# Small unused writes between GpSimd's indirect transfers in a two-layer transformer kernel

## The chip, the cores and the metric

The kernel runs on one core of a Trainium2 chip. The metric is device time in microseconds (us). It is one program with one launch, and its engines are TensorE (PE), VectorE (DVE), ScalarE (ACT), GpSimd (POOL) and SyncE (SP), which work in parallel and wait for one another on semaphores.

## The reference

1024 tokens of width 256 pass through four stages. Each adds its result to its input and normalises the sum.

```
x = layernorm(x + attention(x))          # 16 heads, causal, latent keys of rank 64
x = layernorm(x + experts0(x))           # 64 experts, top 8, at most 128 tokens each
x = layernorm(x + recurrence(x))         # state = tanh(f) * state + g, along the sequence
x = layernorm(x + experts1(x) + shared(x))   # 8 experts, top 2, and one shared MLP

experts0: logits = x @ router.T; the 8 largest probabilities of a token, divided by their sum, weigh
          the outputs of its 8 experts; a token's place in its expert's queue is a running count;
          expert e: silu(xe @ gate) * (xe @ up) @ down      (256 -> 96 -> 256)
experts1: 2 largest of 8, softmax of the two; expert e: silu(x @ w1a) * (x @ w1b) @ w2   (256 -> 512 -> 256)
shared:   silu(x @ w_gate) * (x @ w_up) @ w_down          (256 -> 1024 -> 256)
```

Everything is in float32.

## The kernel before, in words

The tokens form 8 tiles of 128. Every engine runs its own hand-written program, and its order is the order of the code; no scheduler moves anything. GpSimd's program matters here. It does small arithmetic (splitting queries into a high and a low part at L696 and L698, the inverse roots of the layer norms at L703), and it issues all transfers whose addresses depend on the data. Such an indirect transfer takes an index for each of 128 rows out of a tile and moves 128 rows of 1 KB, between on-chip memory and a table in HBM. There are four kinds:

- **First sends** (`send`, L705 to L709). When a tile's attention output is normalised (`x1_rows`), its top 8 experts are known (`send_i`), and eight transfers write its rows into `xe_d`, the table from which experts0 reads. Tiles 0 to 5 issue one transfer in every second slot of the following tile's attention, between splits. The seventh tile (`t == TILES - 2`) issues one a slot, in a stretch where no splits are left, and the last tile issues its eight in one go once attention has ended. After the last tile's k-th send SP loads expert k's rows (the keys are sorted, so expert k's rows are complete by then), and PE starts on expert 0.
- **Home sends** (`send_home`, L733 to L739), one for each of 64 experts, write expert outputs to `ye_d`. The change leaves them alone.
- **Second sends** (L774 to L778): 16 transfers write the rows for experts1 into `xd_d`. SP waits for all of them, then loads the first block of rows. At that time PE computes the shared MLP for the first half of the tokens (`shared_in`, then `shared_out`, L1979); its fourth quarter is preceded by the transposition of the first block (`block_T`, L1988), for which those rows are needed.
- **Final gathers** (L781 to L784): 16 transfers read each token's two expert outputs back from `yd_d`. Meanwhile PE computes the shared MLP's second half (L1625 to L1627), ACT its silu (L957), DVE the product (L1424), and after the third, fourth and further products DVE adds a tile's gathered rows (`last_sum`, L1560 and L1562). Four variances follow and then the last norms.

The inverse root of the last tile (`rstd_of(TILES - 1)`, L703) stands in GpSimd's program behind the seventh tile's sends; behind it come that tile's norm, its routing and its sends.

Of the kernel before, what the change touches and what calls it, by code (L numbers as in the profile page):

```python
# [6 lines left out]
P = 128  # L7
T, HID = 1024, 256
TILES = T // P
# [7 lines left out]
E0, TOP0, CAP, I0 = 64, 8, 128, 96  # L17
# [19 lines left out]
def build(nc, x, xT, wq, wq_ropeT, wkv_aT, kv_ln, wkv_b, woT, router0T, gate_up0, down0, w_in, init_state,  # L37
# [5 lines left out]
    with ctx:  # L43
        def sb(name, shape, dt=f32):
            return ctx.enter_context(nc.sbuf_tensor(name, shape, dt))

        def sem(name):
            return ctx.enter_context(nc.semaphore(name))
# [60 lines left out]
        rsum = sb("rsum", [P, 3, QUAD])  # L109
        rinv = sb("rinv", [P, 3, QUAD])  # L110
        y = sb("y", [P, HID])
        sgd = sb("sgd", [P, 2, BANK])
        ctxT = sgd
        stats = sb("stats", [P, 6])
# [111 lines left out]
        def out_of(n):  # L226
# [28 lines left out]
            sem(n) for n in ("zeroed", "x1T_psd", "x1T_done", "logits_done", "logits_read", "chosen_done",  # L255
                             "place_done", "place_read", "send_done"))
        sent = [sem(f"sent0_{u}") for u in range(2)]
        last_sends = sem("last_sends")
        consts0, route_step, exp_ready, exp_done, winv_done = (
            sem(n) for n in ("consts0", "route_step", "exp_ready", "exp_done", "winv_done"))  # L260
# [118 lines left out]
        def tile_of(G):  # L379
            return G // SETS  # L380
# [269 lines left out]
        def _(pool):  # L650
# [39 lines left out]
            def split_q(m):  # L690

                qt, h = divmod(2 * m, HEADS)
                two = qT[:, h * T:(h + 2) * T].rearrange("p (h t) -> p h t", h=2)[:, :, qt * P:(qt + 1) * P]
                if m >= 3:
                    pool.wait_ge(scores_ready, 2 * (m - 3) + 2)
                pool.tensor_copy(q_his[m % 3], two).then_inc(q_half, 1)  # L696
                pool.wait_ge(q_half, m + 1)
                pool.tensor_tensor(q_los[m % 3], two, q_his[m % 3].bitcast(f32), ALU.subtract).then_inc(q_split, 1)  # L698

            def rstd_of(k, s=0):  # L700

                pool.wait_ge(var_done, k + 1)
                pool.tensor_tensor(rstd[:, s:s + 1], mv[:, s, 1:2], minus_half[:, 0:1], ALU.pow).then_inc(rstd_done, 1)  # L703

            def send(t, k):  # L705
                pool.wait_ge(send_done, t + 1)
                pool.wait_ge(exp_done, t + 1)
                pool.indirect_dma_start(xe_d, bass.IndirectOffsetOnAxis(send_i[:, t, k:k + 1], 0), x1_rows[:, t, :],  # L708
                                        None).then_inc(sent[k % 2] if t < TILES - 1 else sent_last[k], 16)  # L709
# [7 lines left out]
            def pool_slot(G, i, n):  # L717
                if n % 2 == 0 and n // 2 + 3 < TILES * PAIRS:
                    split_q(n // 2 + 3)
                t, at = divmod(n - 2 * HEADS, HEADS)  # L720
                if t == 0 and at == 0:
                    pool.wait_ge(homes_made, 2)
                    pool.wait_ge(rows_zeroed, 16 * ROWS_ZEROED)
                if 0 <= t < TILES - 1 and (t < TILES - 2 and at % 2 or t == TILES - 2 and at < TOP0):
                    send(t, at // 2 if t < TILES - 2 else at)
                if SETS + 2 <= G < GROUPS and (G % SETS, i) == (2, 0):
                    rstd_of(tile_of(G) - 1)
            head_slots(pool_slot)
            rstd_of(TILES - 1)
            for k in range(TOP0):  # L730
                send(TILES - 1, k)
                pool.sem_inc(last_sends, 1)

            def send_home(e, u):

                hold(pool, ye_done, e + 1)
                hold(pool, home_done, e + 2 - u % 2)
                pool.indirect_dma_start(ye_d, bass.IndirectOffsetOnAxis(home_i[:, u:u + 1], 0),  # L738
                                        ye[:, u, :], None).then_inc(moved[u], 16)  # L739
# [35 lines left out]
            for t in range(TILES):  # L775
                for k in range(TOP1):
                    pool.indirect_dma_start(xd_d, bass.IndirectOffsetOnAxis(slot1[:, t, k:k + 1], 0),
                                            x1[:, t, :], None).then_inc(sent1, 16)  # L778
            pool.wait_ge(st_yd[0], 16 * (BLOCKS - BLOCKS // 2))
            pool.wait_ge(st_yd[1], 16 * (BLOCKS // 2))  # L780
            for t in range(TILES):  # L781
                for k in range(TOP1):
                    pool.indirect_dma_start(last_rows[:, t, k, :], None, yd_d,  # L783
                                            bass.IndirectOffsetOnAxis(slot1[:, t, k:k + 1], 0)).then_inc(moved[t], 16)  # L784
            for t in range(TILES // 2):
                rstd_of(3 * TILES + t, t)

# [1321 lines left out]
```

## Time and profile before

| | us |
|---|---|
| median of 3 runs | 816.11 |
| lowest and highest run | 810.94 and 816.73 |
| profiled execution, first to last instruction | 851.6 |
| mean granted clock of PE in it | 0.982 |

The profiled execution's own span is 35.5 us longer than the median run. Only that execution has a trace, so every duration below is one of it.

### The profile page before, as it was taken

How to read it: one execution, taken by the hardware profiler on the slowest of the kernel's cores; microseconds unless marked ns; L12 is line 12 of the kernel's file. 1: busy time of each engine (PE TensorE's matmuls, PEld its weight loads, DVE VectorE, ACT ScalarE, POOL GpSimd, SP SyncE). 2: the span in 40 equal slices, each digit the busy share in tenths (PEclk: the TensorE clock that was granted, in tenths of full speed). 3: DMA queues.
4: the chain of work that ended last, by engine and by line, in shares of the span. 5: the costliest groups of instructions: out<-in, count | busy, mean ns of one | idle time of the engine just before them, and what ended most of it. 6: DMA issues, size and time to landing. Idle time of an engine off the chain costs nothing.

```text
span 851.6 us, 16159 instructions
## 1 busy us (share of the span) xinstructions
PE 786.6 (92%) x4635; PEld 660.7 (78%) x4635; DVE 556.9 (65%) x1423; ACT 394.8 (46%) x898; POOL 271.2 (32%) x357
## 2 busy tenths in 40 slices
PE   8998999999899999999879998899999799999957
PEld 7887877778787887777677877788897688888746
DVE  4324778877778787777345555468856387778536
ACT  1334656656565666655123343323333266666411
POOL 2004445534333232222345545524415100000241
PEclk9999999999999999999889999999999999999979
DMA  7449950000000000073176999687621335555321
GB/s 212 102 107 384 406 198 34 34 27 27 21 27 28 20 21 14 27 240 135 51 230 184 323 319 296 213 288 257 246 99 69 106 112 150 149 149 153 95 69 49
DMA packets 62881, 120.74 MB, mean 142 GB/s; under 512 B 18272, under 2 KB 32864, under 8 KB 62688
## 3 DMA queue, kind: packets, MB, share of 16 engines
q1 hardware_dynamic: 51824, 95.41, 35.2%
q0 software_dynamic: 7680, 21.51, 7.0%
q10 hardware_dynamic: 3312, 3.02, 1.0%
q8 instruction: 33, 0.54, 0.3%
q14 instruction: 32, 0.26, 0.1%
HBM read 76.13 MB, written 43.78 MB: 141 GB/s over the span
## 4 chain that ended last, share of the span: by engine, by line
PE 65%; DVE 11%; issue 11%; ACT 4%; POOL 3%; another core or an unknown queue 3%; DMA 2%; DVEq 0%; SPq 0%; ACTq 0%; POOLq 0%
PE scores L1627 9%; PE scores L1625 8%; PE scores L1626 8%; PE scores L1849 5%; PE acc_ps L2035 4%; PE misc_ps L1755 3%; PE probsT_ps L1762 3%; PE probsT_ps L1740 3%; PE misc_ps L1753 3%; DVE xT_lo L1096 3%; PE scores L1859 3%; PE acc_ps L1740 2%; PE probsT_ps L1979 2%; DVE neg_max L1090 2%
## 5 line engine op out<-in xcount | busy, mean ns | idle before, releaser
L826 ACT ACTIVATE area<-scores,neg_max 128x128 f32<-128x128 f32 (+7 forms) x128 | 94.9, 742 | 87.7 <-DVE neg_max L1090 85.5
L1090 DVE TENSOR_REDUCE neg_max<-scores 128x1 f32<-128x128 f32 (+7 forms) x128 | 95.8, 750 | 22.1 <-PE scores L1712 20.8
L708 POOL DMA_INDIRECT xe_d<-x_rows,send_i x64 | 64.1, 1001 | 55.5 <-ACT x_rows L850 38.5
L738 POOL DMA_INDIRECT ye_d<-area,home_i x64 | 61.4, 959 | 58.7 <-issue 28.6
L1849 PE MATMUL scores<-area 128*96 128x128 f32 x512 | 69.1, 279 | 2.1 <-issue 1.3
L1625 PE MATMUL scores<-kT_hi,weff_hi 128*128 128x512 f32 (+3 forms) x172 | 66.8, 388 | 0.9 <-ACT area L803 0.4
L1849 PEld LDWEIGHTS scores<-area 128*96 128x96 f32 x512 | 60.5, 166 | 5.2 <-issue 2.7
L1627 PE MATMUL scores<-kT_hi,weff_lo 128*128 128x512 f32 (+3 forms) x172 | 61.7, 359 | 0.0
L1626 PE MATMUL scores<-kT_lo,weff_hi 128*128 128x512 f32 (+3 forms) x172 | 61.5, 358 | 0.0
L696 POOL CAST weff_hi<-area 128x256 fp32r<-128x256 f32 x42 | 17.0, 406 | 136.5 <-PE scores L1712 88.8
L1755 PE MATMUL misc_ps<-xT_lo,xT_hi 128*128 128x512 f32 x144 | 58.4, 406 | 2.2 <-DVE xT_lo L1096 2.1
L783 POOL DMA_INDIRECT area<-yd_d,slot x16 | 15.3, 955 | 141.0 <-DMA yd_d<-area 136.4
L1740 PE MATMUL probsT_ps<-ident,area 128*128 128x128 f32 x320 | 48.6, 276 | 5.3 <-DVE xT_lo L1096 5.1
L1762 PE MATMUL probsT_ps<-area,sgd 128*128 128x256 f32 x162 | 50.5, 395 | 1.3 <-ACT sgd L839 0.9
L1859 PE MATMUL scores<-area 96*128 96x256 f32 x128 | 40.6, 399 | 11.0 <-DVE area L1268 9.6
L874 ACT ACTIVATE area<-scores 96x128 f32<-96x128 f32 x64 | 17.3, 271 | 67.7 <-PE scores L1849 40.3
L1096 DVE TENSOR_TENSOR xT_lo<-probsT_ps,xT_hi 128x512 fp32r<-128x512 f32 x53 | 36.1, 686 | 18.5 <-ACT xT_hi L833 17.5
L1753 PE MATMUL misc_ps<-xT_hi 128*128 128x512 f32 x96 | 47.4, 494 | 0.1
L1625 PE MATMUL scores<-xT_hi,weff_hi 128*128 128x512 f32 x110 | 46.1, 419 | 0.0
L1268 DVE TENSOR_TENSOR area<-area,scores 96x128 f32<-96x128 f32 x64 | 18.0, 282 | 41.1 <-ACT area L874 26.1
L1740 PEld LDWEIGHTS probsT_ps<-ident,area 128*128 128x128 f32 x320 | 36.0, 143 | 11.1 <-issue 8.1
L2035 PE MATMUL acc_ps<-area 128*128 128x256 f32 x184 | 43.5, 379 | 0.8 <-DVE area L1511 0.8
(290 smaller groups left out, 2081.4 us busy)
## 6 DMA issues: line engine op xcount, KB each, us to landing
area<-w SPq DMA_DIRECT2D x23, 512.0 KB, 4.0
area<-gate_up SPq DMA_DIRECT2D x24, 384.0 KB
xe_d<-area SPq DMA_DIRECT2D x8, 1088.0 KB, 11.3
ye_d<-area SPq DMA_DIRECT2D x8, 1024.0 KB, 16.7
area<-w SPq DMA_DIRECT2D x8, 1024.0 KB, 7.2
area<-ye_d SPq DMA_DIRECT2D x15, 512.0 KB, 5.2
area<-xe_d SPq DMA_DIRECT2D x28, 272.0 KB
area<-down SPq DMA_DIRECT2D x24, 192.0 KB
```

What stands on the lines that cost most here:

```text
L826: act.activation(row_of(n)[:, 0:L], score_bank(n)[:, 0:L], ACT.Exp, bias=neg_max[:, n % 4:n % 4 + 1], accum_out=rsum[:, s, k:k + 1]).then_ ...
L1090: dve.tensor_reduce(neg_max[:, n % 4:n % 4 + 1], score_bank(n)[:, 0:(n // HEADS + 1) * P], AX.X, ALU.max, negate=True).then_inc(max_ready, 1)
L1625: pe.matmul(out_ap, lh, rh, start=start, stop=False)
L1626: pe.matmul(out_ap, lh, rl, start=False, stop=False)
L1627: return pe.matmul(out_ap, ll, rh, start=False, stop=stop)
L1740: last = pe.transpose(seat_of("block", b)[:, i * P:(i + 1) * P], row_of(QUAD * G + i)[:, k * P:(k + 1) * P], ident[:])
L1753: pe.matmul(ctx_ps[:], latent[:, k, :], pT_hi[b % 3], start=k == 0, stop=False)
L1755: pe.matmul(ctx_ps[:], latent[:, k, :], pT_lo[b % 3], start=False, stop=k == tile_of(G)).then_inc(ctx_step, 1)
L1762: pe.matmul(out_of(n), ctxT[:, G % 2, i * P:(i + 1) * P], wvo[:, h * HID:(h + 1) * HID], start=True, stop=True).then_inc(out_ready, 1)
L1849: last = pe.matmul(half[b][0:I0, part * P:(part + 1) * P], weights_of(e)[0][:, c, part * I0:(part + 1) * I0], xeT[:, b, c, :], start=c == ...
L1859: pe.matmul(half[2 + b][:, 0:HID], hT[:, b, :], weights_of(e)[1], start=True, stop=True).then_inc(ye_ps, 1)
L2035: last = pe.matmul(acc[:, 0:HID], hdT[:, u, c * P:(c + 1) * P], w2_b[:, u, c, :], start=c == 0, stop=c == I1 // P - 1)
```

## The change

A tile `breath` of 128 x 256 is added, and a helper that sets some of its columns to zero and then makes GpSimd wait for its own write. Nothing reads the tile. The helper is called after each of the seventh tile's eight sends (twice, 256 columns), after the last tile's sends except the eighth (128 columns), after each of the 16 second sends (128 columns) and after each of the 16 final gathers (256 columns). That is 16 + 7 + 16 + 16 = 55 writes. The instructions that were there keep their order on every engine.

```diff
+        breath = sb("breath", [P, HID])
...
+            def breathe(columns):
+
+                pool.memset(breath[:, 0:columns], 0.0).then_inc(breathed, 1)
+                breaths[0] += 1
+                pool.wait_ge(breathed, breaths[0])
...
                     send(t, at // 2 if t < TILES - 2 else at)
+                    if t == TILES - 2:
+                        breathe(HID)
+                        breathe(HID)
...
             for k in range(TOP0):
                 send(TILES - 1, k)
                 pool.sem_inc(last_sends, 1)
+                if k < TOP0 - 1:
+                    breathe(P)
...
                     pool.indirect_dma_start(xd_d, bass.IndirectOffsetOnAxis(slot1[:, t, k:k + 1], 0),
                                             x1[:, t, :], None).then_inc(sent1, 16)
+                    breathe(P)
...
                     pool.indirect_dma_start(last_rows[:, t, k, :], None, yd_d,
                                             bass.IndirectOffsetOnAxis(slot1[:, t, k:k + 1], 0)).then_inc(moved[t], 16)
+                    breathe(HID)
```

GpSimd's own program around the seventh and the last tile's sends, before. The names after the operation are the tile written and the tiles read, in brackets stand the semaphores waited for, and x12 is twelve alike in a row (the last four of the sixth tile and the eight of the seventh):

```order
L703 TENSOR_TENSOR rstd<-mv,minus_half 128x1 [waits var_done]
L708 DMA xe_d<-x_rows,send_i 65536x272 [waits exp_done,send_done] x12
L703 TENSOR_TENSOR rstd<-mv,minus_half 128x1 [waits var_done]
L708 DMA xe_d<-x_rows,send_i 65536x272 [waits exp_done,send_done] x8
L738 DMA ye_d<-area,home_i 16384x256 [waits zeroed,ye_done,home_done]
```

The same place in the changed kernel, from the seventh tile's last send on (L718 is the send, L705 the inverse root):

```order
L718 DMA xe_d<-x_rows,send_i 65536x272 [waits exp_done,send_done,breathed]
L711 MEMSET breath 128x256
L711 MEMSET breath 128x256 [waits breathed]
L705 TENSOR_TENSOR rstd<-mv,minus_half 128x1 [waits var_done,breathed]
L718 DMA xe_d<-x_rows,send_i 65536x272 [waits exp_done,send_done]
L711 MEMSET breath 128x128
L718 DMA xe_d<-x_rows,send_i 65536x272 [waits exp_done,send_done,breathed]
```

Two writes now stand between the seventh tile's sends and ahead of the last tile's inverse root, and one between the last tile's sends; each transfer behind a write waits for `breathed`.

GpSimd's program at the second sends and the final gathers, before:

```order
L703 TENSOR_TENSOR rstd<-mv,minus_half 128x1 [waits var_done]
L777 DMA xd_d<-x_rows,slot 2944x256 [waits slots1_ready]
L777 DMA xd_d<-x_rows,slot 2944x256 x15
L783 DMA area<-yd_d,slot 128x256 [waits st_yd1,st_yd0]
L783 DMA area<-yd_d,slot 128x256 x15
L703 TENSOR_TENSOR rstd<-mv,minus_half 128x1 [waits var_done] x4
```

In the changed kernel, from the last second send on (L792 is the second send, L799 the gather):

```order
L792 DMA xd_d<-x_rows,slot 2944x256 [waits breathed]
L711 MEMSET breath 128x128
L799 DMA area<-yd_d,slot 128x256 [waits st_yd1,st_yd0,breathed]
L711 MEMSET breath 128x256
L799 DMA area<-yd_d,slot 128x256 [waits breathed]
```

The two runs of 16 transfers are no longer unbroken: a write with its wait stands after every one.

## Rows read from the trace of the kernel before

**Rows 1.** The page: the span, and each engine's busy time, share and instructions.
```profile
span 851.6 us, 16159 instructions
PE 786.6 (92%) x4635; PEld 660.7 (78%) x4635; DVE 556.9 (65%) x1423; ACT 394.8 (46%) x898; POOL 271.2 (32%) x357
```

**Rows 2.** The chain that ended last: start, length (us) and what it is.
```profile
405.29 2.10 issue
...
421.62 11.12 another core or an unknown queue
...
460.83 2.31 another core or an unknown queue
...
659.91 7.21 another core or an unknown queue
...
813.86 8.99 issue
```

**Rows 3.** Timeline, last tile's sends: start, us, engine, what, [idle before <-releaser].
```profile
420.88 0.17 DVE L1189 TENSOR_SCALAR send_i<-keys_i 128x8 int32<-128x8 int32 x1
421.34 1.04 POOL L708 DMA_INDIRECT xe_d<-x_rows,send_i  x1 [5.08 <-DVE send_i L1189]
...
427.75 1.04 PE L1849 MATMUL scores<-area 128*96 128x128 f32 x8
...
430.26 0.96 POOL L708 DMA_INDIRECT xe_d<-x_rows,send_i  x1 [0.30 <-issue]
432.77 0.44 ACT L874 ACTIVATE area<-scores 96x128 f32<-96x128 f32 x2 [11.14 <-remote]
```

**Rows 4.** Timeline, second sends and the first block of experts1.
```profile
663.70 0.96 POOL L777 DMA_INDIRECT xd_d<-x_rows,slot  x1 [0.30 <-issue]
666.17 0.81 SPq L614 DMA_DIRECT2D area<-xd_d  x2
...
672.96 0.38 PE L1988 MATMUL misc_ps<-ident,area 128*128 128x128 f32 x2
```

**Rows 5.** Timeline, final gathers and the shared MLP's second half.
```profile
812.25 0.39 PE L1627 MATMUL scores<-xT_hi,kT_lo 128*128 128x512 f32 x1
...
819.99 0.95 POOL L783 DMA_INDIRECT area<-yd_d,slot  x1 [0.30 <-issue]
822.23 0.60 ACT L957 ACTIVATE sgd<-scores 128x512 f32<-128x512 f32 x1 [10.08 <-remote]
...
824.27 0.80 PE L1625 MATMUL scores<-xT_hi,kT_hi 128*128 128x512 f32 x1 [8.21 <-DVE kT_lo L1410]
...
835.27 0.48 DVE L1560 SCALAR_TENSOR_TENSOR area<-area,weight,x_rows 128x256 f32<-128x256 f32 x1
```

**Rows 6.** Windows: PE, PEld, DVE, ACT, POOL busy us (count); granted clock, DMA share, GB/s.
```profile
432.60:439.50 6.90, 6.09 (x24) 5.51 (x25) 2.71 (x12) 1.66 (x5) 1.43 (x2) 0.51 0.73 205
...
818.30:828.50 10.20, 4.23 (x10) 3.36 (x11) 4.39 (x10) 2.39 (x6) 2.02 (x3) 0.50 0.14 43
```

**Rows 7.** Groups and timeline: GpSimd's writes, a send among splits, a home send.
```profile
L662 POOL MEMSET area<- 128x1024 f32 x1 | 1.0, 952 | 0.0
...
L651 POOL MEMSET ident<- 128x128 f32 x1 | 0.2, 204 | 0.3 <-POOLq L2099 0.3
...
122.07 1.01 POOL L708 DMA_INDIRECT xe_d<-x_rows,send_i  x1 [0.15 <-issue]
123.08 0.41 POOL L696 CAST q_hi<-area 128x256 fp32r<-128x256 f32 x1
...
437.65 0.47 ACT L881 ACTIVATE area<-scores,hw 128x256 f32<-128x256 f32 x1 [0.58 <-PE scores L1859]
439.03 0.96 POOL L738 DMA_INDIRECT ye_d<-area,home_i  x1 [2.04 <-ACT area L881]
```

**Rows 8.** Timeline of GpSimd: the seventh tile's first send and the inverse root behind its sends.
```profile
398.22 0.96 POOL L708 DMA_INDIRECT xe_d<-x_rows,send_i  x1 [24.01 <-ACT x_rows L850]
...
415.69 0.57 POOL L703 TENSOR_TENSOR rstd<-mv,minus_half 128x1 f32<-128x1 f32 x1 [7.66 <-DVE mv L1122]
```

More of the change, by code:

```diff
@@ L257, in build @@
         sent = [sem(f"sent0_{u}") for u in range(2)]
+        breathed = sem("breathed")
         last_sends = sem("last_sends")
@@ L703, in rstd_of @@
                 pool.tensor_tensor(rstd[:, s:s + 1], mv[:, s, 1:2], minus_half[:, 0:1], ALU.pow).then_inc(rstd_done, 1)
+            breaths = [0]
+            def breathe(columns):
+                pool.memset(breath[:, 0:columns], 0.0).then_inc(breathed, 1)
+                breaths[0] += 1
+                pool.wait_ge(breathed, breaths[0])
             def send(t, k):
```

## The prediction

> **What bounds the kernel.** The page comes first: PE is busy in 92% of an 851.6 us span [rows 1], so time is lost where PE is made to stand, and GpSimd, busy in 32%, matters only where somebody waits for it. The chain of waits comes next. Most of it is work; I looked for long pieces that are none, and four of the longest lie beside the four runs of indirect transfers that the change touches: 2.10 us from 405.29, 11.12 from 421.62, 7.21 from 659.91 and 8.99 from 813.86 [rows 2]. The timeline of such a piece shows what it is. PE ends expert 0's gate and up products at 428.79 (427.75 + 1.04), and ACT, which has nothing else to do, starts on them at 432.77; the row calls the releaser "remote", which is to say that no record of the increment was found [rows 3]. GpSimd's eighth send ended at 431.22, 1.55 us ahead. It is the same with the gathers: PE's chunk ends at 812.65, ACT starts on it at 822.23, 1.29 us after GpSimd's last gather has ended at 820.94 [rows 5]. At the second sends the chain stands from 659.91 to 667.12, and GpSimd's last send ended at 664.66 [rows 2, 4]. So in the profiled execution PE's signals to ACT and DVE are held back while GpSimd issues indirect transfers one behind another, and come when the run is over. The hold isn't there from the start of a run: the piece at 659.91 begins some 15 us after the first of those sends (663.70 less 15 intervals of 1.26 is 644.8).
>
> **What the holds cost there.** At the last tile 432.77 - 428.79 = 4.0 us, and then PE works at a granted 0.51 (the 1.2 GHz level) from 432.6 to 439.5, 6.09 us busy [rows 6], of which half, 3.0, is lost: 7.0. At the seventh tile 2.1 [rows 2], and a stretch at the lower clock behind it, for which I take somewhat less than the last tile's 3.0, since part of it is idle filler: 4.5 in all. At the second sends the first block's rows can't be loaded before 666.17, when SP has seen all sends land, 2.47 us after the last one started at 663.70 [rows 4]; with 2.5 us for the load as well, PE could transpose at 668.7 instead of 672.96, and with a slower load at 670: 3 to 4, say 3.5. At the gathers PE stands 8.21 us before 824.27, and half of 4.23 us at clock 0.50 is 2.1 [rows 5, 6]: 10.3. Together 25.3 us. In experts0 the chain has four more such pieces, 2.31 us at 460.83 and three alike of 2.33 to 2.42 [rows 2], 9.4 us in all, and the change adds nothing there. All holds make 34.7 us.
>
> **Where I chose: are the holds in the timed runs?** The profiled execution took 851.6 us first to last instruction, the median of the timed runs is 816.11. That is 35.5 us less, though a time holds all that the span holds. The holds add up to 34.7, nearly the same. The simplest reading is that the timed runs hold back few of PE's signals or none: what is slow is the recorded execution. The missing records of the increments speak for that too: recording is what is overloaded there. I give this 60% or so. Against it, something else in recording may cost 35 us evenly, and then the holds are real.
>
> The Trainium skill (Runtime: NRT & Kernel Launch, The ~15µs preamble/postamble breakdown) speaks to the same gap: a profile's total time is about 6.2 us longer than the reported execution time, whatever the kernel. By that rule 845 of the 851.6 us should have shown in the runs; this case's 35.5 us disagree, and by the rule 29.3 us would be peculiar to this kernel, still more than the 25.3 us beside the four runs.
>
> **The change part by part.** It removes nothing and moves nothing; it adds 55 writes and 55 waits of GpSimd for itself. *The price of one.* A 128-column write takes 204 ns, a 1024-column one 952 [rows 7]; between them 0.83 ns a column, so 256 columns take 0.31 us. A GpSimd instruction can start as a transfer ends (122.07 + 1.01 = 123.08 [rows 7]): 0.00 to 0.01 us. From the end of what it waits for to a transfer's start I take the 0.29 us between DVE's `send_i` (ends 421.05) and the first send (421.34) [rows 3]. A send now comes every 0.96 + 0.01 + 0.20 + 0.29 = 1.46 us instead of 0.96 + 0.30 = 1.26 [rows 3]: 0.20 more. A gather comes every 0.95 + 0.01 + 0.31 + 0.29 = 1.56 instead of 1.25 [rows 5]: 0.31 more. From below: a transfer can follow an instruction after 0.15 us [rows 7], so 0.06 and 0.17. From above: a home send started at 439.03, 0.91 us after the end of the ACT result that it waits for (437.65 + 0.47 [rows 7]), so 0.82 and 0.93. I take 0.20 and 0.31, since there too a transfer carries the wait itself, as here.
>
> *Seventh tile.* Two writes a send: 0.96 + 0.01 + 0.31 + 0.08 + 0.31 + 0.29 = 1.96 us a send (0.08 is my estimate of the second write's wait, the smallest gap of such kind in GpSimd's splits). From 398.22 the run ends with its last writes at 398.22 + 7 x 1.96 + 1.67 = 413.6; before it ended at 408.0. The inverse root behind it started at 415.69 [rows 8], so in an execution with holds it is covered. Without holds that root is due 4.5 us earlier, at 411.2, and waits 2.4 us for GpSimd, on the path: norm, routing and sends of the last tile stand behind it. **+2.4** (0 to 2.4).
>
> *Last tile.* Seven writes, the k-th send 0.2 k later. PE needs about 1.5 us an expert at full clock, no less than 1.46. The eighth send is 1.4 us later, and home sends, of which eight may be outstanding, catch up. **0** (to +1).
>
> *Second sends.* 15 writes stand ahead of the last send, and SP, then PE, wait for it. Without holds PE has three quarters of `shared_out` to do, until about 664, and stands anyway: nothing hides it. 15 x 0.20 = **+3.0** (0.9 to 12.3).
>
> *Gathers.* The last starts 15 x 0.31 = 4.7 later, at 824.6, and lands, with the 2.47 us of a send, at 827.1. DVE starts to add the last tile's rows at 835.27 in the record [rows 5], without holds 10.3 earlier, at 825.0. So it waits **+2.1** (0 to 11), and the four variances and last norms behind it move.
>
> DVE and PE get no instruction. The sum without holds is 2.4 + 0 + 3.0 + 2.1 = 7.5 us, and 816.1 + 7.5 = **823.6**, a rise of 0.9%. The bounds of the price alone give 817 to 828, leaving out the upper end, which is a rival below.
>
> The Trainium skill (SBUF — State Buffer, Who interferes with whom) says that a GpSimd instruction that only writes isn't held by a DVE instruction with two SBUF inputs; no row of before has a write beside DVE work, so none here shows it. If it were wrong, the writes would last as long as DVE's, 0.4 to 0.7 us, and the sum would double.
>
> **The rivals.** *Holds are real and the writes end them.* The timed runs lose 25.3 us beside the four runs, and a pause every 1.4 us lets PE's signals through. For it: home sends with gaps between them show holds of 2.3 us at most, while unbroken runs show 4 to 10. Against it: the 35.5 us. It gives 816.1 - 25.3 + 7.5 = 798, down to 795 if the seventh tile's cost stays covered. *Real in part, or ended in part*: half of it, 816.1 - 12.6 + 7.5 = 811, from 805 to 815; home sends already have pauses of 0.3 to 2 us and still show holds, so the pause might not be enough. Second sends then cost 12.3, gathers 15 x 0.93 = 14 less 2.6 of slack = 11.4, the seventh tile 5: 29 us, 845. It decides from an interval of about 1.7 us on, where each 0.1 us costs 3 us. Against it: in the trace transfers carry their waits. *It does nothing*: writes lie in the 0.30 us pause between transfers; 815 to 819.
>
> **How the numbers follow.** No holds and the priced writes: 48%, 819 to 828. Holds ended: 20%, 795 to 804. In part: 16%, 805 to 816. Nothing: 11%. Costly wait: 5%, above 830. Three runs of before lie within 5.8 us, so 1%, 8.2 us, is about what a measurement tells from no change: the bounds are 807.9 and 824.3. Faster: 20% and 5 of the 16, so 25%. Slower: 5% and 24 of the 48, 29%. Same: 46%. The two signs share the cases, so the likeliest one's own range, 819 to 828, stands beside the whole one, 801 to 828, which leaves out some 10% below and 9% above.
>
> **What would show it.** In the changed kernel's profile I expect the holds to be shorter or gone, whatever the time does: its span should fall by 10 to 20 us towards the timed median, while the median doesn't. Sends every 1.4 to 1.5 us, gathers every 1.5 to 1.6, MEMSET rows of 0.20 and 0.31 us. Interval of 2 us: the costly wait. The prediction is wrong if the median falls with the span; then the holds were in the timed runs, and the 35.5 us had another cause.

## The result, and the profile after

| | before | changed |
|---|---|---|
| median of 4 runs, us | 814.87 | 833.46 |
| lowest and highest | 810.94, 816.73 | 829.36, 837.68 |
| profiled execution, first to last instruction | 851.6 | 831.3 |
| its own time | not recorded | 833.02 |

The ratio is 1.0216, 95% interval 1.0174 to 1.0259: the changed kernel is **18.6 us slower** by the medians (17.6 by the ratio), while its recorded span is 20.3 us shorter than that of before [rows 1]. The profile of before and the times beside it can't be of the same thing. The experiments point to the reason: that profile looks like those taken on one kind of chip, and the times are those of another kind. On which chip it was taken isn't on record.

The page of the changed kernel, the lines that answer to [rows 1], and the shares of the chain by engine:

```profile
span 831.3 us, 16216 instructions
PE 779.6 (94%) x4635; PEld 660.0 (79%) x4635; DVE 557.3 (67%) x1423; ACT 397.9 (48%) x898; POOL 287.9 (35%) x412
PE 65%; POOL 9%; issue 9%; DVE 9%; DMA 4%; ACT 2%; SPq 1%; DVEq 0%; POOLq 0%; ACTq 0%
```

None of the chain's pieces "another core or an unknown queue" of [rows 2] is left, also not those in experts0, where nothing was added. GpSimd's share of the chain is 9%, where it was 3%. At three places somebody waits for it.

*Seventh tile.* The timeline of the changed kernel behind that tile's seventh send (start, us, engine, what, in brackets the idle time before and what ended it):

```profile
411.47 0.15 DVE L1139 TENSOR_SCALAR mv<-mv 128x1 f32<-128x1 f32 x1
411.49 0.97 POOL L718 DMA_INDIRECT xe_d<-x_rows,send_i  x1 [0.45 <-POOL breath L711]
412.45 0.69 POOL L711 MEMSET breath<- 128x256 f32 x2
413.60 0.96 POOL L718 DMA_INDIRECT xe_d<-x_rows,send_i  x1 [0.45 <-POOL breath L711]
414.56 0.69 POOL L711 MEMSET breath<- 128x256 f32 x2
415.34 0.57 POOL L705 TENSOR_TENSOR rstd<-mv,minus_half 128x1 f32<-128x1 f32 x1
416.41 0.69 PE L1786 MATMUL scores<-ident,x_rows 128*128 128x128 f32 x2 [4.98 <-DVE x_rows L1143]
```

The variance is there at 411.47 + 0.15 = 411.62, its inverse root starts at 415.34, 3.72 us later, because almost all of one send, a second send and four writes still stand ahead of it in GpSimd's program. PE has stood 4.98 us.

*Second sends.* The last of them and the first block's rows:

```profile
652.11 0.96 POOL L792 DMA_INDIRECT xd_d<-x_rows,slot  x1 [0.28 <-POOL breath L711]
653.07 0.22 POOL L711 MEMSET breath<- 128x128 f32 x1
654.57 0.82 SPq L616 DMA_DIRECT2D area<-xd_d  x2
656.58 0.44 PE L2005 MATMUL misc_ps<-ident,area 128*128 128x128 f32 x2 [4.10 <-DMA area<-xd_d]
656.85 5.31 PE L1996 MATMUL probsT_ps<-area 128*128 128x256 f32 x16
```

The load leaves 654.57 - 652.11 = 2.46 us after the last send started, as before (2.47 [rows 4]); PE stands 4.10 us for it.

*Gathers.* The last one, the last rows' addition, and the 32 products of PE that wait for it:

```profile
810.38 1.04 POOL L799 DMA_INDIRECT area<-yd_d,slot  x1 [0.27 <-POOL breath L711]
813.22 0.48 DVE L1577 SCALAR_TENSOR_TENSOR area<-area,weight,x_rows 128x256 f32<-128x256 f32 x1 [2.11 <-DMA area<-yd_d,slot]
818.05 8.86 PE L1996 MATMUL probsT_ps<-area 128*128 128x256 f32 x32 [5.22 <-DVE area L1590]
```

Windows of the changed kernel: GpSimd alone at work, and then three stretches, each behind a stand of PE (columns as in [rows 6]):

```profile
411.70:415.90 4.20, 0.00 (x0) 0.00 (x0) 0.00 (x0) 0.00 (x0) 3.55 (x7) 0.94 0.18 66
416.30:421.00 4.70, 4.59 (x23) 4.53 (x23) 1.77 (x12) 0.98 (x4) 0.00 (x0) 0.50 0.00 0
656.30:661.90 5.60, 5.32 (x18) 4.42 (x19) 0.76 (x2) 0.37 (x1) 0.00 (x0) 0.70 0.64 215
817.70:826.40 8.70, 8.35 (x31) 7.04 (x32) 5.07 (x17) 2.16 (x4) 0.55 (x1) 0.80 0.27 90
```

After stands of 4.98, 4.10 and 5.22 us PE works at a mean granted clock of 0.50 (the 1.2 GHz level throughout), 0.70 and 0.80 (part of the stretch at that level). The prediction has such a term for the holds, and none for the delays that the writes themselves bring.

### The profile page after: what moved, and what is told of

It is laid out like the page before. It is cut to its first block, busy times and chain, and to the rows that moved or that the text cites. A ratio compares the mean times of both kernels' runs of the same rounds, so it can differ in the third digit from the quotient of the medians.

```text
span 831.3 us, 16216 instructions
## 1 busy us (share of the span) xinstructions
PE 779.6 (94%) x4635; PEld 660.0 (79%) x4635; DVE 557.3 (67%) x1423; ACT 397.9 (48%) x898; POOL 287.9 (35%) x412
## 4 chain that ended last, share of the span: by engine, by line
PE 65%; POOL 9%; issue 9%; DVE 9%; DMA 4%; ACT 2%; SPq 1%; DVEq 0%; POOLq 0%; ACTq 0%
PE scores L1644 8%; PE scores L1643 8%; PE scores L1642 8%; PE scores L1866 6%; PE acc_ps L2052 5%; PE misc_ps L1772 4%; PE probsT_ps L1757 3%; PE misc_ps L1770 3%; PE probsT_ps L1779 3%; PE scores L1876 3%; PE acc_ps L1757 2%; DVE xT_lo L1113 2%; POOL xd_d L792 2%; POOL area L799 2%; POOL breath L711 2%
## 5 line engine op out<-in xcount | busy, mean ns | idle before, releaser
L718 POOL DMA_INDIRECT xe_d<-x_rows,send_i x64 | 64.2, 1003 | 57.5 <-ACT x_rows L867 38.5
L1866 PE MATMUL scores<-area 128*96 128x128 f32 x512 | 66.8, 273 | 1.2 <-DVE area L1279 1.0
L799 POOL DMA_INDIRECT area<-yd_d,slot x16 | 15.9, 996 | 137.3 <-DMA yd_d<-area 133.2
L1113 DVE TENSOR_TENSOR xT_lo<-probsT_ps,xT_hi 128x512 fp32r<-128x512 f32 x53 | 36.1, 686 | 18.7 <-ACT xT_hi L850 18.5
L1644 PE MATMUL scores<-xT_hi,weff_lo 128*128 128x512 f32 x110 | 43.3, 394 | 0.0
L1643 PE MATMUL scores<-xT_lo,weff_hi 128*128 128x512 f32 x110 | 43.1, 392 | 0.0
L891 ACT ACTIVATE area<-scores 96x128 f32<-96x128 f32 x64 | 17.5, 273 | 51.8 <-PE scores L1866 51.8
```

Source lines behind the costliest of these rows:

```text
L1643: pe.matmul(out_ap, lh, rl, start=False, stop=False)
L1644: return pe.matmul(out_ap, ll, rh, start=False, stop=stop)
L1866: last = pe.matmul(half[b][0:I0, part * P:(part + 1) * P], weights_of(e)[0][:, c, part * I0:(part + 1) * I0], xeT[:, b, c, :], start=c == ...
```

## The experiments

Eighteen runs follow, of eleven different kernels, in five groups; all of a group ran on one chip, beside the kernel before. There the kernel before took 858.7 (e0 to e3), 816.2 (e4, e5), 859.0 (e6 to e9), 857.4 (e10 to e13) and 816.7 us (e14 to e17). I call a chip on which it takes about 858 a *holding* chip, after what the trace shows there. The first and the fourth group came to the same chip, with two others in between, and it held both times; so four chips were seen, two of each kind. That the difference belongs to the chip, and not to the hour, rests on these few.

**The kernel before, unchanged** (e0, holding chip).

> The kernel before, unchanged: its own profiled execution, with that execution's own time beside its span, and repeated timings. Theory (held-back signals belong to one recorded execution and not to the others): timed 811 to 818, ratio 1.00; if the profiled execution again spans over 845 us, its time will stand apart from the timed ones; if it spans about 813, no piece of 4 us or more in which ACT or DVE wait for a signal without a record stands at the last tile or the gathers. Rival (holds are in every execution, and the profile's 35 us are something else): the same holds of 4.0 us at the last tile and 9 to 10 us at the gathers in an execution whose own time is about 815.

Measured: 856.6 us (853.3 to 862.3), ratio 0.9987 (0.9957 to 1.0016); the profiled execution took 858.04, span 856.0. Both readings set down before had expected about 815 and missed. Its last send at the last tile, and the first work of ACT behind it:

```profile
432.69 0.96 POOL L708 DMA_INDIRECT xe_d<-x_rows,send_i  x1 [0.30 <-issue]
435.41 0.44 ACT L874 ACTIVATE area<-scores 96x128 f32<-96x128 f32 x2 [11.38 <-remote]
...
826.90 0.60 ACT L957 ACTIVATE sgd<-scores 128x512 f32<-128x512 f32 x1 [11.48 <-remote]
```

It is the picture of [rows 3, 5], in an execution whose own time, 858.04, lies among those of the twelve timed ones. So the holds are no matter of one recorded execution: on this chip every execution pays for them. The profile of before (851.6) fits these chips; the three times beside it (810.9 to 816.7) fit the others.

**The parts alone, on holding chips** (e1 to e3, e7 to e9, e10 to e12). Each is the changed kernel with the helper called at one place. For the seventh tile:

```diff
                     if t == TILES - 2:
                         breathe(HID)
                         breathe(HID)
...
-                if k < TOP0 - 1:
-                    breathe(P)
...
-                    breathe(P)
...
-                    breathe(HID)
```

> Only the seventh tile's 16 writes of 256 columns; no writes at the last tile, the second sends and the gathers. Theory (each write delays GpSimd, and the last tile's inverse root stands behind the writes; the changed kernel's trace shows it start 3.7 us after its variance was there): +3.5 to +4.5 us, 818.4 to 819.4. Rival 1 (the term of the prediction, +2.4): 817.3. Rival 2 (a pause that comes while the sends are in flight also drops PE's clock or moves the start of the experts further): +6 or more.

> Only the seventh tile's 16 writes, again. On a chip where before takes about 816: the inverse root waits 3.64 us for GpSimd (trace of the whole change: ready 411.68, start 415.32), and PE, which stood 4.98 us, then works at its lower clock, 1.2 us more; theory +4.8, 821. Prediction's term: +2.4, 818.6. Rival (the root's delay is absorbed behind the last tile's sends): +1 or less. On a chip where before takes about 858: -1.5 as measured.

> Only the seventh tile's 16 writes. Where before takes about 816: theory +4.8 (root 3.64 us late, then 1.2 us at PE's lower clock), 821; the prediction's term +2.4. Where before takes about 858: 0 to -1.8, as twice measured.

Measured: 0.9972 (0.9949 to 0.9995), 0.9999 (0.9971 to 1.0026), 1.0023 (0.9991 to 1.0056). Nothing on balance. Every price expected of a chip without holds (+2.4 and more) failed here, and the later expectations for such a chip were merely taken from earlier results. The traces show what was exchanged: from the seventh tile's first send to the last tile's first send a holding chip takes 23.1 to 25.2 us without these writes and 23.0 to 23.4 with them, a chip without holds 18.5 to 18.7 without them.

The second sends alone (only the call behind the transfer into `xd_d` is kept):

> Only the 16 writes of 128 columns behind the second sends. Theory (15 intervals longer by 0.20 to 0.23 us, the last send 3.0 to 3.4 us later, nothing hides it): +3.0 to +3.5 us, 818. Rival (the extra standing of PE before the first block also brings its lower clock level, which the following product pays for at half speed): +5 to +6. Rival 2 (hidden by shared_out, which is still running): 0.

> Only the 16 writes behind the second sends, again. On a chip where before takes about 816: 15 intervals longer by 0.20 are 3.0, and PE, which stands 4.14 instead of 1.18 us before the first block's transposes, does 16 products in 5.30 instead of 3.62 us behind it, 1.7 more; theory +4.7, 821. Prediction's term: +3.0, 819. On a chip where before takes about 858: 0 as measured.

> Only the 16 writes behind the second sends. Where before takes about 816: theory +4.7 (3.0 of interval and 1.7 of PE's lower clock), 821; the prediction's term +3.0. Where before takes about 858: 0 to -1, as twice measured.

Measured: 0.9991 (0.9962 to 1.0021), 0.9992 (0.9968 to 1.0016), 1.0024 (0.9997 to 1.0051). Nothing, where e2 expected +3.0 to +3.5. The chain's piece at the second sends (7.26 us where the writes are one column long, below) is gone from the trace of e2, but PE stands 4.12 us before 677.30 all the same, now for the later rows (their load starts at 675.26, in e0 at 671.32): one wait took the place of the other. A 0 was set down too, for another reason (the writes hidden by `shared_out`), and that reason isn't what the trace shows.

The gathers alone (only the call behind the transfer out of `yd_d`):

> Only the 16 writes of 256 columns behind the final gathers. Prediction's term: +2.1 us, 817. Theory from the changed kernel's trace (16 intervals of 1.55 instead of 1.26, no cover left, since the last gathers' rows were waited for by DVE before as well): +4.5 to +5.0, 819.5. Rival (DVE shares something with the writes, or PE's clock falls behind the longer stand): +7 or more, which the sum of the four parts would need to reach the 18.6 us of the whole change.

> Only the 16 writes behind the final gathers, again. On a chip where before takes about 816: the last rows are added 3.5 us later, and PE, which then has stood 5.21 instead of 1.12 us, does its next 32 products in 8.70 instead of 7.17, 1.5 more; theory +5.0, 821. Prediction's term: +2.1, 818. On a chip where before takes about 858: -9 to -10 as measured.

> Only the 16 writes behind the final gathers. Where before takes about 816: theory +5.0 (last rows 3.5 us later, 1.5 of PE's lower clock), 821; the prediction's term +2.1. Where before takes about 858: -8 to -10, as twice measured.

Measured: 0.9889 (0.9852 to 0.9927), 0.9905 (0.9873 to 0.9938), 0.9920 (0.9887 to 0.9954): 7 to 10 us faster. In the first of them what was expected (slower by 2 to 5, or 7) failed: the prediction's first rival is true here. Its terms even give the number, 10.3 us of hold less 2.1 for the writes, 8.2, but that is luck in part: from the first gather to the end e0 takes 51.7 us, e3 45.1 and e5, without holds or writes there, 39.5, so in these traces the hold is worth 12.2 and the writes 5.6. The other two expectations only repeat the measurement.

**The whole change again** (e4 on a chip without holds, e6 on a holding one), no edit.

> The whole change again, beside the kernel before on the same chip. In the four runs just done on one chip the kernel before took 858.7 us, not 814.9, and gathers' writes alone made it 9 us faster: so the holds are in timed executions there. Theory (whether holds are there depends on the chip or the session, and the writes end them where they are): where before takes about 858, the change gives 830 to 840, faster by some 20 to 28 us; where before takes about 815, it gives 830 to 835, slower. Rival (the holds depend on something else and the change always costs 18 us): 877 beside 858.

> The whole change a third time, beside its parts on one chip, so that the parts can be added up. Two chips have been seen: one on which the kernel before takes 858.7 us and its trace shows the holds, and one on which it takes 816.2 and the trace of a kernel nearly the same shows none. Theory: where before takes about 816, +17 us, ratio 1.021, and the parts add up to it. Where before takes about 858: the holds beside all four runs go, 830 to 845. Rival (on such a chip the holds move elsewhere): 850 or more.

Measured: e4 833.6 beside 816.2, ratio 1.0215 (1.0184 to 1.0247), which repeats the result; e6 849.1 beside 859.0, ratio 0.9877 (0.9837 to 0.9918), by the ratio 10.6 us *faster*. The same two programs stand in the opposite order on the two kinds of chip. e6 fell between its two readings (845 at most, 850 or more): the holds beside the four runs went, and those in experts0, which the change leaves alone, stayed; the chain of e6:

```profile
452.37 2.40 another core or an unknown queue
461.55 2.29 another core or an unknown queue
...
526.28 3.22 another core or an unknown queue
```

From the first to the last home send e6 takes 547.60 - 432.07 = 115.5 us, e4 532.89 - 433.76 = 99.1.

**The last tile alone** (e5, chip without holds; only the call behind the last tile's sends is kept).

> Only the last tile's seven writes of 128 columns. Theory: where before takes about 858 us, the hold of 4.0 us and the half-clock stretch behind it (3.0 us) go, and the sends' delay of up to 1.4 us comes: -5 to -7 us. Where before takes about 815: +0 to +1.4. Rival (PE's lower clock isn't from the hold): -2 to -4.

Measured: 815.2 beside 816.2, ratio 0.9988 (0.9967 to 1.0009): nothing. Its trace is worth more than its time: with a span of 812.3 us it is the first of a kernel nearly that of before on a chip without holds, with no hold in its chain, and gives what the prediction had to guess. In the order of the three places above:

```profile
410.22 0.15 DVE L1134 TENSOR_SCALAR mv<-mv 128x1 f32<-128x1 f32 x1
410.46 0.57 POOL L705 TENSOR_TENSOR rstd<-mv,minus_half 128x1 f32<-128x1 f32 x1 [3.04 <-DVE mv L1134]
644.95 0.44 PE L2000 MATMUL misc_ps<-ident,area 128*128 128x128 f32 x2 [1.18 <-DMA area<-xd_d]
645.22 3.62 PE L1991 MATMUL probsT_ps<-area 128*128 128x256 f32 x16
791.98 1.10 POOL L795 DMA_INDIRECT area<-yd_d,slot  x1 [0.30 <-issue]
795.99 0.48 DVE L1572 SCALAR_TENSOR_TENSOR area<-area,weight,x_rows 128x256 f32<-128x256 f32 x1
800.81 7.17 PE L1991 MATMUL probsT_ps<-area 128*128 128x256 f32 x32 [1.12 <-DVE area L1585]
```

and its windows behind the same three places:

```profile
411.50:416.10 4.60, 4.25 (x35) 3.93 (x36) 2.65 (x16) 1.67 (x4) 0.00 (x0) 1.00 0.00 0
645.00:648.90 3.90, 3.90 (x21) 3.44 (x22) 0.75 (x2) 0.37 (x1) 0.00 (x0) 1.00 0.70 198
800.80:808.00 7.20, 7.17 (x32) 6.00 (x32) 4.76 (x16) 2.16 (x4) 0.23 (x1) 1.00 0.33 109
```

The root starts 0.09 us after its variance; PE stands 1.18 and 1.12 us, and its clock is 1.00 in all three. Between first instructions of GpSimd the two traces compare as follows (us):

| from, to | last tile's writes only | whole change | more |
|---|---|---|---|
| start, seventh tile's first send | 397.61 | 398.85 | 1.2 |
| to the last tile's first send | 18.50 | 23.33 | **4.8** |
| to the last home send | 110.05 | 111.30 | 1.3 |
| to the first second send | 94.41 | 95.80 | 1.4 |
| to the first gather | 152.26 | 157.23 | **5.0** |
| to the end of the span | 39.47 | 44.79 | **5.3** |

The bold rows hold the writes, 15.1 of the 19.0 us. The first row can't be the writes' doing, since no write has run by then; over all profiled executions of this study it varies from 396.1 to 399.8. The other two, 2.7 us together, lie in what varies as well: over the seven traces without holds the stretch from the last home send to the first second send takes 93.7 to 96.4 us, both ends in kernels (e14, e15) that have no write in it. The bold rows are steadier: the whole change again (e4) has 23.34 us in the first of them, and e14 to e17, without the two long writes, 18.5 to 18.7.

**Second sends and gathers together** (e17, chip without holds; the calls at the seventh and the last tile are left out).

```diff
-                    if t == TILES - 2:
-                        breathe(HID)
-                        breathe(HID)
...
-                if k < TOP0 - 1:
-                    breathe(P)
```

> The writes behind the second sends (128 columns) and the final gathers (256) together, none at the seventh and the last tile. Where before takes about 816: +9 to +10 us by the traces' differences (4.7 and 5.0), by the prediction's terms +5.1. Where before takes about 858: -9, the sum of the two parts as measured there.

Measured: 826.5 beside 816.7, ratio 1.0126 (1.0097 to 1.0154), 10.3 us (7.9 to 12.6). The traces' sum (+9 to +10) holds, the prediction's terms (+5.1) lie below the interval. PE stands 4.16 us before the first block, as in the whole change, and its 16 products take 5.21. Behind the gathers the 32 products take longer still than in the whole change (8.86), after a stand as long:

```profile
809.16 9.95 PE L1991 MATMUL probsT_ps<-area 128*128 128x256 f32 x32 [5.13 <-DVE area L1585]
```

Where PE works at clock 1.00 they take 7.17 (e5), so what such a stand costs behind it isn't fixed: 1.7 us there, 2.8 here, and 2.2 to 3.0 in e3, e9 and e12 (9.40 to 10.21 us behind stands of 4.4 to 4.5).

With 17.5 for the whole (e4) and nothing for the last tile, the difference leaves some 7 us to the seventh tile (3 to 11 by the intervals); the trace's 4.8 lies within. That tile was never timed alone on a chip without holds.

**The length of the write** (e13, holding chip): `breathe(1)` at all four places.

> The whole change with one column in place of 128 and 256: the same 55 writes and waits, each write as short as can be. If the length of the write makes the cost: where before takes about 816, intervals of 1.26 to 1.35 us, +0 to +6, at most 822. If the wait makes it: intervals of 1.4 us or more, +12 or more. Where before takes about 858: if the wait alone ends the holds, 842 to 848, some 3 to 5 us better than the whole change (849); if the pause has to be long, 853 to 858.

Measured: 847.0 beside 857.4, ratio 0.9900 (0.9837 to 0.9962). A one-column write takes 0.11 us, and sends come every 1.35 us:

```profile
421.83 0.96 POOL L718 DMA_INDIRECT xe_d<-x_rows,send_i  x1 [0.28 <-issue]
422.79 0.11 POOL L711 MEMSET breath<- 128x1 f32 x1
423.18 0.96 POOL L718 DMA_INDIRECT xe_d<-x_rows,send_i  x1 [0.28 <-issue]
```

Its chain has the holds at the last tile and the second sends still, at full length, and a shorter one at the gathers; there sends and gathers come every 1.33 to 1.35 us:

```profile
418.84 11.93 another core or an unknown queue
...
659.60 7.26 another core or an unknown queue
819.76 4.53 another core or an unknown queue
```

With 128 columns, an interval of 1.46 us (1.55 at the gathers), those three are gone (e6). So on a holding chip the wait alone isn't enough at such intervals; whether it's the longer interval or the longer write that ends the holds, these two kernels don't tell apart. The seventh tile speaks for the interval: there two one-column writes make it 1.89 us, and the last tile's first send comes 20.95 us after the seventh's first (419.04 - 398.09) instead of 24.45 (e0). Of the two readings set down before, the time fits the first, and at the last tile and the second sends the trace fits the second.

**Writes behind the home sends** (e14), and in places that seemed covered (e15, e16). The edit of e14 against the kernel before (the tile and the helper come with it, as in the change):

```diff
...
                 pool.indirect_dma_start(ye_d, bass.IndirectOffsetOnAxis(home_i[:, u:u + 1], 0),
                                         ye[:, u, :], None).then_inc(moved[u], 16)
+                breathe(P)
```

e15 adds to that

```diff
                     send(t, at // 2 if t < TILES - 2 else at)
+                    if t == TILES - 2 and at < TOP0 - 1:
+                        breathe(P)
...
                 pool.sem_inc(last_sends, 1)
+                if k < TOP0 - 1:
+                    breathe(P)
```

and e16 a `breathe(P)` behind each gather as well.

> Only one write of 128 columns behind each of the 64 home sends, none elsewhere. Where before takes about 858 us: theory (writes between indirect transfers end holds) the home sends take 99 to 102 us instead of 114 to 115, -12 to -16 us, 844. Rival (there a hold comes every fourth expert although sends are 1.53 us apart, so a pause doesn't help): 0. Where before takes about 816: 64 x 0.49 us of GpSimd lie in pauses of 0.57 us, so 0 to +2.

> Writes of 128 columns only where the trace without holds has cover: one behind each of the seventh tile's sends except the eighth, behind the last tile's sends except the eighth, and behind each home send; none at the second sends and the gathers. Where before takes about 816: 0 to +2 us. Where before takes about 858: -20 to -26 (home sends 15, last tile 5 to 7, seventh tile 1 to 4), 832 to 838. Rival (as of e14): -5 to -8.

> As the kernel just described, with one write of 128 columns behind each gather as well. Where before takes about 858: 8 to 10 us better than that one, 824 to 829, 4% faster than before. Where before takes about 816: 15 intervals longer by 0.20, of which 1.1 us are covered, and 1.5 us of PE's lower clock: +3.5.

They came to a chip without holds (before: 816.7), so whether writes end the holds in experts0 wasn't tried. All three were expected within a few us of before. Measured: e14 848.8, ratio 1.0404 (1.0369 to 1.0438); e15 848.7, 1.0386 (1.0358 to 1.0413); e16 852.9, 1.0429 (1.0398 to 1.0460). Two of the differences are as expected: e15 against e14, with writes at the seventh and the last tile as well, nothing (in its trace GpSimd has stood 1.63 us when the seventh tile's root comes, so nothing waits for it); e16 against e15, the gathers' writes, 3.5 to 4.2. But the home sends' writes, in all three, were a bad miss: 0 to +2 expected, +32 found. GpSimd's timeline in e14:

```profile
461.22 0.97 POOL L748 DMA_INDIRECT ye_d<-area,home_i  x1 [0.92 <-POOL breath L711]
462.19 0.22 POOL L711 MEMSET breath<- 128x128 f32 x1
463.32 0.97 POOL L748 DMA_INDIRECT ye_d<-area,home_i  x1 [0.92 <-POOL breath L711]
```

A home send comes every 2.10 us, not 1.46, and PE is slowed to that pace from 1.53 us an expert: 64 x (2.10 - 1.53) = 36, and from the first to the last home send the traces have 134.4 us in e14 and 99.6 in e17. The records of GpSimd's semaphore instructions, which the timeline leaves out, show what happens in between (start and duration in ns):

```
e14:  462189  218  MEMSET          e5:  449547  958  transfer
      462442   43  semaphore            450223   17  semaphore
      462564   17  semaphore            450319   17  semaphore
      463323  966  transfer             451076  960  transfer
```

A home send is preceded by two waits that are instructions of their own. Without a write the second has ended 0.17 us before the transfer ahead of it has; behind a write both come after the write, and the transfer starts 0.76 us after the second of them in both columns. It is the prediction's costly wait, at a place that the change had left alone.

At the seventh tile, too, the interval is longer than predicted, 2.11 us and not 1.96: a send there starts 0.45 us behind the second write. Between its two writes stands such a semaphore instruction, at 412.822 in the changed kernel, and the next send starts at 413.596, 0.77 us later. But that instruction alone doesn't cost this: in e15, with one write between the seventh tile's sends, it stands 0.23 us ahead of the send, and at the last tile 0.11, and both send every 1.46 to 1.47 us. What decides between the two prices isn't shown. At the last tile, the second sends and the gathers the transfer itself carries the wait for the write and starts 0.27 to 0.28 us behind it (0.29 predicted).

## Why the prediction was wrong, step by step

The case chosen was the one that occurred, signals in time and writes that cost; the step that failed is its sum. The writes were priced at 7.5 us and cost 15.1 in the traces, because the prediction put PE's lower clock behind the stands that the writes lengthen at nothing (4.6), reckoned the root's wait behind the seventh tile's sends too short (1.2) and the cover at the gathers too thick (1.4). One by one:

- **What the 35.5 us are.** "What is slow is the recorded execution" is wrong, and so is the argument from missing records: in e0 they are missing in an execution whose own time is as long. The holds cost time on some chips and were not seen on others; the profile and the three times shown with it fit different kinds. The consequence drawn for the timed runs, that they hold nothing, is right for the chip of the result, but by luck: on two of the four chips of the experiments it would have been wrong, and the first rival occurs there. The size of the holds was also short: holding chips are 42 us slower, not 34.7, and of the rest most lies in the home sends (114.4 us in e0 against 99.6 in e17: 15, where the chain's pieces had given 9.4).
- **The price of a write** was right: 0.22 and 0.31 to 0.33 us for 0.20 and 0.31, the last tile's sends every 1.46 to 1.47 us (1.46), the second sends +0.20 each, the gathers +0.31.
- **Seventh tile, +2.4**: measured +4.8. The root was 3.6 us later than in e5 (2.4 predicted), of which 7 x 0.15 = 1.1 is the interval; the remaining 1.2 us are PE, which at clock 0.50 takes 6.84 us from the root to the first send (415.34 to 422.18) where e5 takes 5.65 (410.46 to 416.11).
- **Last tile, 0**: right (e5: 0.9988; e15).
- **Second sends, +3.0**: measured +5.0. The added stand, 4.10 - 1.18 = 2.9, is the term; the 16 products behind it take 5.31 instead of 3.62 us, 1.7 more; 0.4 stays open.
- **Gathers, +2.1**: measured +5.3. The run of gathers grew by 4.7 as reckoned. The cover wasn't 2.6: in e5 the last rows are added 795.99 - 791.98 = 4.0 us after the last gather starts, in the changed kernel 2.8, so it was 1.2, and 3.5 remain. The 32 products behind take 8.86 instead of 7.17: 1.7.
- **The sum.** 4.8 + 0 + 5.0 + 5.3 = 15.1 for 7.5. Of the 7.6 missing, 1.2 + 1.7 + 1.7 = 4.6 is one omitted term at three places: *a stand of PE made longer is paid again in its clock afterwards*. The prediction counted that for holds (3.0 and 2.1 us) and not for its own delays. It is a reading of the windows (clock 1.00 behind stands of 1.1 to 1.4 us, 0.50 to 0.80 behind those of 4 to 5); no run varied the stand alone. The seventh tile's longer wait gives 1.2 and the gathers' thinner cover 1.4. Against the timed difference (18.6 by the medians here, 17.5 by the ratio in e4, there 15.0 to 20.2) 2.4 to 3.5 us are left, in stretches without writes and in the scatter of executions, and stay open.
- **The costly wait**, given 5%, is real at the home sends in e14 (2.10 us). At the four places of the change it isn't, but for 0.15 us an interval at the seventh tile; the 2.11 us there say nothing by the rival's bound of 1.7, since the cheap price already gave 1.96.
- **What would show it.** The span fell by 20.3 us while the median rose, about as written down (10 to 20, and the median not falling). Its meaning was misread: not the change but, most likely, another kind of chip made the span shorter. The page that the prediction set beside the gap is about something else. The Trainium skill (Runtime: NRT & Kernel Launch, The ~15µs preamble/postamble breakdown) gives its 6.2 us for a profile's total time, and 851.6 is the span from first to last instruction, so it doesn't bear on that gap. No run here shows a total time; the execution of 833.02 us has a span of 831.3, 1.7 less.
- **Writes beside DVE work**, on which the sum would have doubled, cost nothing. In e17 a 256-column write takes 0.33 us while DVE subtracts two tiles that both lie in SBUF (`split_weights`, L1422), as long as in the changed kernel where DVE stands (0.33 at 811.42):

```profile
790.00 0.76 DVE L1422 TENSOR_TENSOR kT_lo<-area,kT_hi 128x256 fp32r<-128x256 f32 x2
790.01 0.33 POOL L711 MEMSET breath<- 128x256 f32 x1
```

  The other page drawn on says so (the Trainium skill, SBUF — State Buffer, Who interferes with whom), and the trace agrees.

What gives the holding chips their holds isn't known; no run here varies that. Nor is there a trace of the kernel before itself on a chip without holds: e5 stands for it, with a time 1.0 us less (ratio 0.9988).

## What to carry to other kernels

Before a profile is explained by its gap to the timed runs, have one execution's own time and span side by side, on the same chip. A delay in front of TensorE is priced twice: the stand, and what its clock loses behind it, here 1.2 to 3.0 us for a stand that grew from about 1 to between 4 and 5 us. And price a filler between transfers at each place where it goes: the same 128-column write added 0.20 us to an interval at the second sends and 0.57 at the home sends, where two waits that used to be over early came to stand behind it.

## What the hardware showed unexpectedly

- The same kernel takes 814.9 to 816.7 us on some chips and 857.4 to 859.0 on others, each execution within 1% of its chip's median, and a change ranks as 2.2% slower on the one and 1.2% faster on the other.
- On holding chips signals of PE to ACT are held back up to 9.6 us (812.65 to 822.23 [rows 5]) in runs of indirect transfers 1.26 us apart; holds of several us stay at 1.35 (e13), and in e6 none is left where the transfers are 1.46 apart with a longer write between them; yet shorter holds, 2.3 to 3.2 us, occur among home sends whose median distance is 1.5.
- GpSimd stood idle for 0.57 us of every 1.53 between home sends, and a write of 0.22 us put there lengthened the interval to 2.10: each home send started 0.76 us after the second of its two semaphore instructions, with the write and without it.
